# Clamped distances of the attention stage moved from VectorE to GpSimd in a graph-attention and expert kernel

## What is computed

```
hW = h @ W
hp, hm = (adj > 0) @ hW, (adj < 0) @ hW
e_plus = leaky_relu(concat([hp, hm]) @ a)[:, 0]
att = where(edge_adj > 0, e_plus[None, :], NEG_INF)
att = where(edge_adj < 0, e_minus[None, :], att)
att = softmax(att, axis=1)
edge_support += (att * edge_adj) @ hW          # for each of 3 heads
```

## Time and profile before

| | before |
|---|---|
| median of 3 runs | 1004.78 us |
| lowest and highest | 1002.82, 1010.12 us |
| span of the profiled execution | 1004.0 us, 10398 instructions |
| PE / DVE / ACT / POOL busy | 901.2 / 694.9 / 628.8 / 148.5 us |
| attention stage, chunk 0 (about 261.5 to 302.2) | 40.7 us |
| each of chunks 2 to 6 | 68.4 us (one is 68.5) |
| chunk 1 | 68.9 us |

### The profile page before, as it was taken

One profiled execution on the slowest core, in us unless ns is written; L12 is line 12 of the kernel. 1 busy time (PEld: TensorE's weight loads), 2 busy tenths in 40 slices (PEclk: granted clock), 3 DMA queues, 4 the chain that ended last, 5 costly groups with the idle time before them and its releaser, 6 DMA issues.

```text
span 1004.0 us, 10398 instructions
## 1 busy us (share of the span) xinstructions
PE 901.2 (90%) x2770; PEld 458.4 (46%) x2770; DVE 694.9 (69%) x1287; ACT 628.8 (63%) x922; POOL 148.5 (15%) x184
## 2 busy tenths in 40 slices
PE   5999999899799999999999999999998771587787
PEld 5634343466674344444444444444544331376542
DVE  6523333352799899999999999999667785321234
ACT  2345554511799898998998989989433331564531
POOL 0000000000000000010000001010132555256540
PEclk9999999999899999999999999999999895699989
DMA  9877767220089956645445465220300021455523
GB/s 283 305 249 270 261 228 257 71 87 16 10 214 318 328 180 183 145 120 143 121 121 144 118 179 168 84 104 1 119 1 6 27 72 35 133 145 166 154 98 123
DMA packets 100635, 145.26 MB, mean 145 GB/s; under 512 B 11469, under 2 KB 51079, under 8 KB 99559
## 3 DMA queue, kind: packets, MB, share of 16 engines
q1 hardware_dynamic: 97318, 137.90, 45.5%
q0 software_dynamic: 3264, 6.74, 1.9%
HBM read 122.02 MB, written 22.60 MB: 144 GB/s over the span
## 4 chain that ended last, share of the span: by engine, by line
PE 46%; issue 24%; DVE 19%; ACT 4%; DVEq 3%; POOL 2%; another core or an unknown queue 1%; DMA 1%; SPq 0%; ACTq 0%; POOLq 0%
PE psum L1788 15%; DVE work L1371 9%; PE psum L1906 7%; PE psum L1872 4%; DVE big L1380 3%; PE psum L2093 3%; PE psum L2104 2%; PE psum L2063 2%; DVEq L1371 2%; PE psum L1944 1%; PE psum L1945 1%; PE psum L1771 1%; POOL sorted_dram L703 1%; PE psum L1949 1%; PE psum L1727 1%
## 5 line engine op out<-in xcount | busy, mean ns | idle before, releaser
L1906 PE MATMUL psum<-big,h 128*128 128x512 f32 (+1 forms) x1092 | 444.0, 568 | 13.2 <-DVE big L1380 13.0
L1906 PEld LDWEIGHTS psum<-big,h 128*128 128x128 f32 x1092 | 206.1, 191 | 250.2 <-issue 176.3
L1380 DVE TENSOR_TENSOR big<-work,big 128x1536 f32<-128x1536 f32 (+1 forms) x182 | 299.1, 1643 | 8.3 <-ACT work L886 2.5
L884 ACT ACTIVATE work<-work,shift 128x1024 f32<-128x1024 f32 (+1 forms) x182 | 198.3, 1089 | 42.2 <-DVE work L1371 38.9
L1788 PE MATMUL psum<-big,h 128*128 128x512 f32 x312 | 146.3, 611 | 0.0
L1371 DVE TENSOR_SCALAR work<-rows,h 128x512 f32<-128x512 f32 x312 | 137.1, 482 | 2.8 <-POOLq L678 2.8
L886 ACT ACTIVATE work<-work,shift 128x512 f32<-128x512 f32 (+1 forms) x182 | 123.4, 678 | 0.0
L657 POOL TENSOR_SCALAR_AFFINE_SELECT big<-big 128x128 f32<-128x128 f32 x50 | 25.2, 505 | 633.7 <-DMA big<-adj_cols_dram 631.5
L880 ACT ACTIVATE work<-rows,h 128x512 f32<-128x512 f32 x156 | 110.6, 709 | 0.0
L1788 PEld LDWEIGHTS psum<-big,h 128*128 128x128 f32 x312 | 56.6, 191 | 68.9 <-issue 68.4
L756 ACT ACTIVATE work<-big 128x2048 bf16<-128x2048 f32 (+1 forms) x42 | 75.0, 1786 | 11.9 <-POOLq L670 9.3
(11 more groups left out here) (296 smaller groups left out, 832.8 us busy)
## 6 DMA issues: line engine op xcount, KB each, us to landing
big<-adj_cols_dram SPq DMA_DIRECT2D x30, 2048.0 KB, 8.0
sorted_dram<-zeros SPq DMA_DIRECT2D x15, 910.0 KB, 14.3
big<-adj_cols_dram SPq DMA_DIRECT2D x9, 1024.0 KB, 7.3
big<-adj_cols_dram SPq DMA_DIRECT2D x6, 1536.0 KB, 6.5
rows<-experts_dram SPq DMA_DIRECT2D x29, 257.5 KB
rows<-stats_dram SPq DMA_DIRECT2D x1, 4608.0 KB, 27.2
rows<-stats_dram SPq DMA_DIRECT2D x1, 3840.0 KB, 20.4
rows<-sorted_dram SPq DMA_DIRECT2D x29, 130.0 KB
```

The costliest lines, as they stand in the source:

```text
L884: nc.scalar.activation(both, both, ACT.Exp, bias=shift[:, 0:1], scale=-1.0)
L1380: nc.vector.tensor_tensor(wadj[:, k % 2, :, 0:w], wexp[:, (n + k) % SLOTS, :, 0:w], ring[:, bass.ds(place, 1), 0:w].broadcast_to([128, HEA ...
L1906: done = nc.tensor.matmul(sums[i], h[:, t, 0:H], wadj[:, t % 2 if v == "plain" else 0, i, 0:w], start=t == 0, stop=t == TILES - 1)
```

## The change

In the branch `plain`, the distances of heads 0 and 1 are computed on POOL by the same two tensor_scalar instructions (`distances`), and DVE keeps only the product. POOL counts the new semaphore `g_p` after the pair. The clearing of the diagonal moves into the same POOL queue: the first third is cleared ahead of the first distance, and the next third after the distances of tiles 3, 11 and 20 of each chunk, each time with POOL's wait for that load. POOL now also waits for `f_ready` and reads the flag. ACT issues the relu of head 2 one tile ahead of the exponential, waits for `g_p` and `g_relu`, and takes the exponential of all three heads in one instruction. All loops of this branch on DVE and ACT are written out.

```diff
--- before.py
+++ after.py
@@ -37,6 +37,8 @@
 SLOT = 8
 ROWS = 3
 SLOTS = 4
+LAST = HEADS - 1
+POOL_HEADS = 2
 ALPHA = 0.2
 NEG_INF = -9e15
 LOWEST = -3e38
@@ -106,8 +108,8 @@
 class InOrder:
 
 
-    def __init__(self, engine, semaphore):
-        self.engine, self.semaphore, self.value = engine, semaphore, 0
+    def __init__(self, engine, semaphore, value=0):
+        self.engine, self.semaphore, self.value = engine, semaphore, value
 
     def done(self, instruction):
 
@@ -361,7 +363,7 @@
         d_stored, d_in = sem("d_stored"), [sem("d_in0"), sem("d_in1")]
         g_in = [sem(f"g_in{i}") for i in range(3)]
         g_y, g_e, g_w, g_mm, g_kept = (sem(f"g_{n}") for n in ("y", "e", "w", "mm", "kept"))
-        g_clear, g_relu, g_order_dve = (sem(f"g_{n}") for n in ("clear", "relu", "order_dve"))
+        g_clear, g_relu, g_order_dve, g_p = (sem(f"g_{n}") for n in ("clear", "relu", "order_dve", "p"))
         early_in, t_ready = sem("early_in"), sem("t_ready")
         biases_in, diag_in, kept_in = (sem(n) for n in (
             "biases_in", "diag_in", "kept_in"))
@@ -649,7 +651,7 @@
                                     fill=0.0, base=0, pattern=[[-1, 128]], channel_multiplier=1)\
                 .then_inc(consts, 1)
 
-            def clear_diagonal(c, t, tile):
+            def clear_diagonal(order, c, t, tile):
 
                 c0, w = CHUNKS[c]
                 if c0 <= t * 128 < c0 + w:
@@ -666,16 +668,44 @@
                     if c == 0 and t1 > MAIN:
                         pool.wait_ge(a_in_tail, 16)
                     for t in range(t0, t1):
-                        clear_diagonal(c, t, cols_of(c, t, t + 1).squeeze(1))
+                        clear_diagonal(order, c, t, cols_of(c, t, t + 1).squeeze(1))
                     nc.gpsimd.nop().then_inc(a_clear, 1)
 
-            for c in range(NCH):
-                for third, (t0, t1) in enumerate(THIRDS):
-                    at = (3 * c + third) % 2 * SLOT
-                    pool.wait_ge(g_in[third], (32 if third == 2 else 16) * (c + 1))
-                    for t in range(t0, t1):
-                        clear_diagonal(c, t, ring[:, at + t - t0 if t < t0 + SLOT else SLOT + t - t0, :])
-                    nc.gpsimd.nop().then_inc(g_clear, 1)
+            def clear_third(order, n):
+
+                c, third = n // 3, n % 3
+                t0, t1 = THIRDS[third]
+                at = n % 2 * SLOT
+                pool.wait_ge(g_in[third], (32 if third == 2 else 16) * (c + 1))
+                for t in range(t0, t1):
+                    clear_diagonal(order, c, t, ring[:, at + t - t0 if t < t0 + SLOT else SLOT + t - t0, :])
+                nc.gpsimd.nop().then_inc(g_clear, 1)
+
+            def distances():
+
+                clear_third(plain_order, 0)
+                for c, (c0, w) in enumerate(CHUNKS):
+                    for t in range(TILES):
+                        n = TILES * c + t
+                        if t == 0 and c < len(k_in):
+                            pool.wait_ge(k_in[c], 16)
+                        pool.wait_ge(g_w, n + 1)
+                        for i in range(POOL_HEADS):
+                            last = nc.gpsimd.tensor_scalar(wexp[:, n % SLOTS, i, 0:w], row_of(c, i),
+                                                           h[:, t:t + 1, H + i], 0.0, ALU.subtract, ALU.max)
+                        last.then_inc(g_p, 1)
+                        if t in (3, 11, 20) and 3 * c + t // 8 + 1 < 3 * NCH:
+                            clear_third(plain_order, 3 * c + t // 8 + 1)
+
+            plain_order, signed_order = (InOrder(pool, pool_order, order.value) for _ in range(2))
+            pool.wait_ge(f_ready, 1)
+            signed = pool.value_load(flag[0:1, 0:1])
+            with pool.If(signed > 0):
+                for n in range(3 * NCH):
+                    clear_third(signed_order, n)
+            with pool.Else():
+                distances()
+            order.value = plain_order.value
             pool.wait_ge(sorted_clear, 16 * PARTS)
             pool.wait_ge(g_mm, TILES * NCH + FREE)
             order.done(nc.gpsimd.iota(slot_at, [[1, TILES], [NP, 2]], base=SPARES, channel_multiplier=TILES))
@@ -852,8 +882,6 @@
                 spread(NCH - 1)
                 keep_turned(3, len(GROUPS))
 
-            LAST = HEADS - 1
-
             def exponentials_signed():
 
                 for c, (c0, w) in enumerate(CHUNKS):
@@ -869,30 +897,30 @@
 
             def exponentials_plain():
 
+                def distance(c, t):
+
+                    w = CHUNKS[c][1]
+                    n = TILES * c + t
+                    if t == 0 and c < len(k_in):
+                        act.wait_ge(k_in[c], 16)
+                    act.wait_ge(g_w, n + 1)
+                    nc.scalar.activation(wexp[:, n % SLOTS, LAST, 0:w], row_of(c, LAST), ACT.Relu,
+                                         bias=h[:, t:t + 1, H + SCORES + LAST]).then_inc(g_relu, 1)
+
+                distance(0, 0)
                 for c, (c0, w) in enumerate(CHUNKS):
-
-                    def tile(t, k):
-
-                        n = TILES * c
-                        slot = (n + k) % SLOTS
-                        place = wexp[:, slot, LAST, 0:w]
-                        act.wait_ge(g_w, t + (n + 1))
-                        nc.scalar.activation(place, row_of(c, LAST), ACT.Relu,
-                                             bias=h[:, bass.ds(t, 1), H + SCORES + LAST]).then_inc(g_relu, 1)
-                        act.wait_ge(g_y, t + (n + 1))
-                        both = wexp[:, slot, 0:LAST, 0:w]
-                        nc.scalar.activation(both, both, ACT.Exp, bias=shift[:, 0:1], scale=-1.0)
-                        act.wait_ge(g_relu, t + (n + 1))
+                    for t in range(TILES):
+                        n = TILES * c + t
+                        if t + 1 < TILES:
+                            distance(c, t + 1)
+                        elif c + 1 < NCH:
+                            distance(c + 1, 0)
+                        act.wait_ge(g_p, n + 1)
+                        act.wait_ge(g_relu, n + 1)
+                        place = wexp[:, n % SLOTS, :, 0:w]
                         nc.scalar.activation(place, place, ACT.Exp, bias=shift[:, 0:1], scale=-1.0).then_inc(g_e, 1)
-
-                    if c < len(k_in):
-                        act.wait_ge(k_in[c], 16)
-                    if c == 0:
-                        tiles_by_four(act, 0, SLOT, tile)
-                        keep_rows()
-                        tiles_by_four(act, SLOT, TILES, tile)
-                    else:
-                        tiles_by_four(act, 0, TILES, tile)
+                        if c == 0 and t == SLOT - 1:
+                            keep_rows()
 
             with act.If(signed > 0):
                 keep_support(NCH - 1)
@@ -1362,46 +1390,23 @@
 
                 nc.vector.nop().then_inc(g_w, SLOTS)
 
-                def distance(c, t, k):
-
-                    c0, w = CHUNKS[c]
-                    n = TILES * c
-                    dve.wait_ge(g_w, t + (n + 1))
-                    for i in range(HEADS - 1):
-                        last = nc.vector.tensor_scalar(wexp[:, (n + k) % SLOTS, i, 0:w], row_of(c, i),
-                                                       h[:, bass.ds(t, 1), H + i], 0.0, ALU.subtract, ALU.max)
-                    last.then_inc(g_y, 1)
-
-                def product(c, t, k, place):
-                    c0, w = CHUNKS[c]
-                    n = TILES * c
-                    dve.wait_ge(g_e, t + (n + 1))
-                    dve.wait_ge(g_mm, t + (n + 1))
-                    nc.vector.tensor_tensor(wadj[:, k % 2, :, 0:w], wexp[:, (n + k) % SLOTS, :, 0:w],
-                                            ring[:, bass.ds(place, 1), 0:w].broadcast_to([128, HEADS, w]),
+                def product(c, t, place):
+
+                    w = CHUNKS[c][1]
+                    n = TILES * c + t
+                    dve.wait_ge(g_e, n + 1)
+                    dve.wait_ge(g_mm, n + 1)
+                    nc.vector.tensor_tensor(wadj[:, n % 2, :, 0:w], wexp[:, n % SLOTS, :, 0:w],
+                                            ring[:, place:place + 1, 0:w].broadcast_to([128, HEADS, w]),
                                             ALU.mult).then_inc(g_w, 1)
 
-                dve.wait_ge(k_in[0], 16)
-                distance(0, 0, 0)
                 for c in range(NCH):
                     for first, end, at in stretches(c):
                         if c > 0 and first == SLOT:
                             keep(c - 1)
                         dve.wait_ge(g_clear, 3 * c + min(first // SLOT, 2) + 1)
-                        if end - first < SLOTS:
-                            for t in range(first, end):
-                                if t + 1 < TILES:
-                                    distance(c, t + 1, t + 1)
-                                elif c + 1 < NCH:
-                                    if c + 1 < len(k_in):
```

(10 more changed lines are left out.)

## The result

| | before | changed |
|---|---|---|
| median (4 runs each) | 1005.13 us | 1453.37 us |
| lowest, highest | 1002.82, 1010.12 | 1451.14, 1453.56 |
| span of the profiled execution | 1004.0 | 1451.1 |

The ratio is 1.444 (95% interval 1.440 to 1.449): 448 us slower. The sign was forecast, the size was not: 1075 was predicted, with 1190 as the upper end.

What follows compares the result with a forecast made beforehand. PE was taken to bound the kernel at 2.56 us per tile. At 2.96 per tile, big chunks add 65 us and loads at the start 7, taking the span from 1004.0 to 1076; predicted 1075, range 1012 to 1190.

Steps and rivals of the forecast that it cites:

- a distance costs 0.75 us, with 0.61 and 1.26 as ends: Attention stage: price of one undisturbed 512-element distance on POOL, bounded from its fill, select and tensor_tensor; 1.45 us per pair.
- The turn: Attention tiles: DVE's product holds the SBUF port against POOL's distance for 1.51 us per tile.
- Chunk 0: First attention chunk, 256-column tiles: 1.51 us per tile against 1.57 with start-up, so 0 us extra.
- The clears and load waits of the big chunks: POOL's queue, per big chunk: diagonal clears now on the path 1.3 us, wait for the load after tile 11 1.0 us.
- early loads: POOL's waits for loads in chunks 0 and 1, where many transfers stand ahead: together about 7 us.
- the tile's time is a sum of two engines: Attention tile: product's turn on DVE plus POOL's pair of distances, 1.51 + 1.45 = 2.96 us, against PE's 2.56.
- DVE and ACT are off the path: Attention tile: DVE would need 1.67 us and ACT 2.3 at most, with an exponential of 1.60, below PE's 2.56.
- The load wait in POOL's queue: After tiles 3, 11 and 20 distances queue behind POOL's wait for adj_cols; 1.0 us per big chunk, at tile 11.
- Rival (c): Two-input price: a distance on POOL costs 1.26 us, a tile 4.0, the whole 1250 us; chance 0.12.
- (a): Line rate: a distance on POOL runs at the fill's rate, 0.61 us, a tile 2.66, the whole 1033 us; chance 0.20.
- (b): No turn-taking: distances slip beside the product, PE sets the pace, the whole 1000 us; chance 0.12.
- Rival (d): PE's clock falls to 1.2 GHz from idling, a tile takes 5.1 us on PE, well over 1200 us; chance 0.03.

Runs made afterwards that it cites:

- e1: Changed kernel with POOL's tensor_scalar doing one step (max with constant 0), the score left out of two heads' distances; 1187.0 us.
- e10: Changed kernel with POOL's tensor_scalar doing one step, adding a constant to a row of features, two heads' distances left out; 1187.0 us.
- e3: Changed kernel with a POOL tensor_tensor (row of features plus broadcast constant) replacing each tensor_scalar, two heads' distances left out; 1132.1 us.
- e4: Changed kernel with DVE's product reading its second input from a constant-filled PSUM bank, not the adjacency in SBUF; span 1208.0 us.
- e11: Changed kernel with POOL computing only head 0's distance and DVE head 1's; 1036.3 us, 59 over the kernel before.
- e8: As e7, but in chunks 1 to 6 head 1's distance of seven tiles per chunk is on POOL; 976.1 us, ratio 0.998 to the kernel before.
- e7: Changed kernel with both heads' distances back on DVE and its three readings of finished sums split ahead of tiles 3, 6, 9; 973.8 us, ratio 0.994.

## Why the prediction was wrong

**The step that failed** is the term "a distance costs 0.75 us, with 0.61 and 1.26 as ends" in "What a distance costs on GpSimd". It measured 1.99 us, above the upper end. Three assumptions of it were tested: that the fixed part is 0.17 (it is 0.21 with one step and 0.29 with two: near enough); that a one-input tensor_scalar has the slope of the one-input select, 0.97 ns per element (it has 2.5, e1 and e10); and that a tensor_tensor, having two inputs, bounds it from above (it is the cheaper instruction, 1.03 us in e3). The number of inputs, by which I ordered the rows, does not order the prices on POOL across kinds of instruction. The second step adds 0.45 us and the scalar per partition 0.06. Why tensor_scalar is the slower kind, these runs don't show.

In numbers: a pair costs 3.97 (e4) where I had 1.45, so 156 x 2.52 = 393 us more than predicted. The turn measured 1.30 where I had 1.51: 33 less (I had left out that the end of the distance already under way overlaps the product by 0.3 us). Chunk 0, for which I took 0, cost 39. The clears and load waits of the big chunks, 2.3 us each in my sum, did not show: 14 less. Of the 7 us for early loads nothing showed. 393 - 33 + 39 - 14 - 7 = 378, and the span missed was 1451 - 1076 = 375.

**What held.** That the tile's time is a sum of two engines and not the larger (e4). That DVE and ACT are off the path, with an exponential of 1.57 us where I had 1.60, and that POOL is never at rest in a big chunk (busy 135.23 of 135.50 us). The load wait in POOL's queue was real but not in this kernel: it needs a POOL that is not late (e11, e8). Rival (c) leaned the right way with a distance of 1.26, but its 1250 is still 200 us short; rivals (a) and (b) fell with the price. Rival (d): the clock did fall, to 0.86 over a chunk, but PE was not the bound, so it cost nothing here.

**What was a little off.** PE needs about 66.9 us per chunk and not 66.6 (steps of 0.429, where I had 0.427), so relieving DVE could give about 1.4 and not 1.8 us per chunk. And the written-out loops give 2.4 us, which I had at 0 with a few us as the other end.

**The two rules that the prediction cited.** The Trainium skill, "GPSIMD Engine Reference", section "Engine selection", calls one-input operations roughly line-rate there. The prediction put that at 0.61 us, the rate of a fill. The measurement decides: 1.49 with one step and 1.99 with two, and the two-input add is faster.

The pairing of DVE's product with POOL's distance held: the stretch goes when one input of the product is read from PSUM (e4). The order did not. The Trainium skill, "SBUF — State Buffer", section "Who interferes with whom", says that issue order decides which of the two blocks. The prediction said that the trace of before agrees; for the pairing it does, but in the earlier trace rows the DVE instruction starts first (789.04, POOL's at 789.13), and it is DVE's that takes 1.94 in place of 0.69 while POOL's keeps its 1.28. In e8, at 525.20, POOL's starts first and is the one stretched; in e1, at 498.0, POOL's starts first, keeps its length, and the product grows. So the order of the starts does not tell who gives way, and what does, these runs don't show.

## What to carry to other kernels

Before work moves to another engine, time that very instruction there, in kind and shape; a bound built from other instructions of that engine by counting inputs was off by 1.6 times at its upper end. If the trace shows two engines taking turns, their times nearly add for that pair, and the comparison to make is the sum against the present bound. An engine with DMA waits in its queue should not be given work whose deadline is shorter than the landing time of the load it waits for.

## What the runs showed of the hardware

- On GpSimd, 512 fp32 elements per partition: tensor_scalar 1.99 us with two steps, 1.94 with two steps and constants for both scalars, 1.49 with one step (max and add alike); tensor_tensor with a broadcast second input 1.03. DVE does the two-step one in 482 ns.
- In the changed kernel a two-step POOL tensor_scalar that starts 0.3 us into a DVE tensor_tensor of 1.76 us with both inputs in SBUF is longer by 1.3 us, and the product isn't. Where POOL's starts first, either may grow or both: POOL's alone (4.21 us at 525.20 in e8), the product and not the POOL instruction ahead of it (2.00 and 1.48 us in e1), both (2.48 and 2.16 us at 457.4 in e8). With a POOL tensor_tensor both grow (2.55 and 2.29 us, e3). With one input of the product in PSUM neither does (e4).
- A one-input tensor_scalar of DVE can be held back beside POOL: 806 ns on average in e11 (0.47 to 0.92), 482 without.
- Six fp32 weight-load and matmul steps of 512 columns take 2.57 us at a granted clock of 1.00 (steps of 0.43 us, e7).
